# Layer 0's first two expert blocks fetch only two words per row, and the row buffers take blocks three to five at once

## The reference

```python
router_logits = x_flat @ gate_w
router_probs = jax.nn.softmax(router_logits, axis=-1)
expert_idx = jnp.argmax(router_probs, axis=-1)
expert_w = jnp.take_along_axis(router_probs, expert_idx[:, None], axis=1)[:, 0]
for e in range(NUM_EXPERTS):          # 8
    h = jax.nn.gelu(x_flat @ w1[e] + b1[e], approximate=False)   # 256 -> 1024
    y = h @ w2[e] + b2[e]                                        # 1024 -> 256
    out = out + jnp.where(expert_idx == e, expert_w, 0.0)[:, None] * y
```

## Time and profile before

| | |
|---|---|
| time before | 1849.13 us, median of 3 runs (1848.25 to 1849.85) |
| profiled execution | 1851.53 us |
| its span, first to last instruction | 1849.7 us |
| PE busy | 1609.4 us (87%) |
| DVE, ACT, POOL busy | 58%, 49%, 21% |
| mean granted PE clock | 0.943 of full speed |
| the experts stage of layer 0: from block 0's up projection to the end of the last down projection | 293.4 to 481.3 us |

### The profile page before, as it was taken

The page is one execution under the profiler, slowest core; times in us unless marked ns, Lnnn a source line. Parts: engine busy times, 40 slices in busy tenths (PEclk is TensorE's granted clock), DMA queues, the critical chain, the costliest instruction groups (busy, mean ns, idle before and its releaser), DMA issues.

```text
span 1849.7 us, 27965 instructions
## 1 busy us (share of the span) xinstructions
PE 1609.4 (87%) x9990; PEld 1215.6 (66%) x9998; DVE 1070.8 (58%) x3025; ACT 906.8 (49%) x2034; POOL 379.6 (21%) x480
## 2 busy tenths in 40 slices
PE   6999858999669999999958699999998779995566
PEld 5677637889556676767535667776675468894444
DVE  7767752222356666666667765555555534325887
ACT  4888821222136666666539455555554102223366
POOL 1000014111132323233240100000000342223734
PEclk9999989999879999999978899999999889997878
DMA  9000028889500000000000200000000338893001
GB/s 339 2 1 1 2 92 322 260 291 292 170 1 12 7 7 7 7 1 1 1 1 1 80 12 7 7 7 7 1 1 12 129 124 264 300 352 127 0 12 35
DMA packets 61625, 152.26 MB, mean 82 GB/s; under 512 B 8960, under 2 KB 39696, under 8 KB 55248
## 3 DMA queue, kind: packets, MB, share of 16 engines
q1 hardware_dynamic: 54096, 133.91, 21.9%
q0 software_dynamic: 5280, 14.47, 2.0%
q10 hardware_dynamic: 2112, 2.10, 0.4%
HBM read 133.89 MB, written 24.75 MB: 86 GB/s over the span
## 4 chain that ended last, share of the span: by engine, by line
PE 69%; DVE 15%; ACT 5%; POOL 4%; issue 4%; DMA 2%; POOLq 1%; SPq 0%; DVEq 0%; ACTq 0%
PE bank L1033 8%; PE bank L1456 8%; PE bank L976 8%; PE bank L1510 7%; PE bank L1523 6%; PE bank L1497 5%; PE bank L1460 5%; PE bank L1440 3%; PE bank L679 3%; PE bank L1862 2%; POOL sorted_h L1225 2%; PE bank L695 2%; PE bank L710 1%; ACT p1f L1578 1%; PE bank L616 1%
## 5 line engine op out<-in xcount | busy, mean ns | idle before, releaser
L1707 DVE TENSOR_REDUCE small<-bank 128x1 f32<-128x512 f32 x128 | 82.5, 686 | 108.7 <-PE bank L1510 108.7
L1052 ACT ACTIVATE e2a<-bank,WB 128x128 f32<-128x128 f32 x156 | 44.6, 368 | 178.7 <-PE bank L1033 178.7
L1703 DVE CUSTOM_DVE_ANT_0 p1f<-bank,p1f 128x512 f32<-128x512 f32 x128 | 83.2, 687 | 81.3 <-PE bank L1510 81.3
L1581 ACT ACTIVATE p2f<-bank,small 128x512 f32<-128x512 f32 x128 | 86.9, 683 | 86.2 <-DVE small L1707 86.1
L751 ACT ACTIVATE l<-l,small 128x256 f32<-128x256 f32 x256 | 108.9, 502 | 32.6 <-DVE small L817 32.2
L1578 ACT ACTIVATE p1f<-p1f,small 128x512 f32<-128x512 f32 x128 | 91.2, 714 | 67.9 <-DVE small L1703 67.5
L400 POOL TENSOR_SCALAR rs<-mv 128x4 f32<-128x4 f32 x16 | 3.6, 226 | 567.4 <-DVEq L230 551.7
L817 DVE CUSTOM_DVE_ANT_0 l<-bank,small 128x256 f32<-128x256 f32 x256 | 90.7, 420 | 13.4 <-PE bank L695 12.5
L1456 PE MATMUL bank<-WA,HT 128*128 128x256 f32 x384 | 93.1, 387 | 5.0 <-DVE p1f L1648 5.0
L1592 ACT ACTIVATE p2f<-bank 128x512 f32<-128x512 f32 x128 | 75.2, 598 | 40.5 <-PE bank L1497 39.0
L1052 ACT ACTIVATE e0a<-bank,WB 128x128 f32<-128x128 f32 x128 | 36.6, 368 | 112.7 <-PE bank L1033 112.7
(11 more groups left out here) (402 smaller groups left out, 3949.6 us busy)
## 6 DMA issues: line engine op xcount, KB each, us to landing
WB<-in_L2pack SPq DMA_DIRECT2D x39, 514.0 KB, 5.1
WB<-in_L2pack SPq DMA_DIRECT2D x39, 512.0 KB, 5.7
WB<-in_L0pack SPq DMA_DIRECT2D x16, 1028.0 KB, 6.4
WB<-in_L0pack SPq DMA_DIRECT2D x16, 1024.0 KB, 7.3
e0a<-in_L0pack SPq DMA_DIRECT2D x7, 1028.0 KB, 5.8
e0a<-in_L0pack SPq DMA_DIRECT2D x7, 1024.0 KB, 6.8
sorted_h<-in_blank SPq DMA_DIRECT2D x6, 1032.0 KB, 16.1
e2a<-sorted_h SPq DMA_DIRECT2D x39, 129.0 KB, 5.6
```

Source lines behind the costliest of these rows:

```text
L1581: ins = a.e.activation(P, k.bank(x), ACT.Exp, bias=self.mx[:, m:m + 1], accum_out=self.sm[:, m:m + 1])
```

## The change

In layer 0 only, blocks 0 and 1 no longer fetch their rows. `load_x` for them fetches words 256 and 257 of each row, 128 pieces of 8 bytes, into a small buffer of its own, `place_of`, counted by the flag `a_place`. POOL takes its index for these two blocks from there, and waits for `a_place`. DVE's two copies at block 2 are gone. Since `xs[0]` and `xs[1]` are free from the start, x3 and x4 no longer wait for `xt_d` 3, and SP issues x2, the two place fetches, x3 and x4 together ahead of block 3's down weights. x5 stays behind block 4's down weights. The counts of the row buffers' semaphores (`ax`) are one less in buffers 0 and 1.

```diff
--- before.py
+++ after.py
@@ -889,11 +889,14 @@
         self.beside = ()
         self.cleared = (k.setup.z0, 3) if tag == "e0" else (k.setup.z2, 5)
         self.a_b2 = k.dma("b2", 1)
-        self.ax = [k.dma(f"ex{i}", len(range(i, nt, 3))) for i in range(3)]
+        late = 3 if topk == 1 else 0
+        self.ax = [k.dma(f"ex{i}", len(range(i + late * (i < 2), nt, 3))) for i in range(3)]
         self.a1 = [k.dma(f"ew{i}", len(range(i, nt, nwb))) for i in range(nwb)]
         self.a2 = [k.dma(f"gather{4 + i}", len(range(i, nt, nwb))) for i in range(nwb)]
         self.sc = k.dma("scatter", n // 2), k.dma("ey0", n // 2)
         self.ay = [k.dma(f"ey{i}", len(range(i, nt, 3))) for i in range(3)]
+        if topk == 1:
+            self.a_place = k.dma("gather0", 2)
         self.ag = [k.dma(f"gather{i}", 1) for i in range(4 * topk)]
         f = k.flag
         nq = self.nq = nf // 4
@@ -902,7 +905,7 @@
         self.two = topk == 1
         if self.two:
             self.count256, self.seat = r(256, a=16, b=16), k.HT[:, :, :].rearrange("p c (t n) -> p (c t) n", n=256)
-            self.seated = f("p_cxn", 4)
+            self.seated, self.place_of = f("p_cxn", 4), r(4, i=2, n=2)
         self.routing = f("e_routing", 5)
         self.xt_t, self.xt_d = f("e_xt_t", nt), f("e_xt_d", nt)
         self.up_q, self.gel, self.dn, self.yc = f("up", nt * nq), f("gel", nt * nf), f("down", nt), f("y", nt)
@@ -1007,7 +1010,7 @@
     def turn_pe(self, t, i):
         k, x = self.k, self.xs[i % 3]
         T = k.bank(6 + i % 2)
-        t.wait_ge(self.ax[i % 3], i // 3 + 1)
+        t.wait_ge(self.ax[i % 3], i // 3 + (0 if self.two and i % 3 < 2 else 1))
         t.wait_ge(self.xt_d, i - 1)
         t.wait_ge(self.routing, self.GATED)
         if self.biased(i) is not None:
@@ -1198,10 +1201,6 @@
             return
         v.wait_ge(self.xt_t, i + 1)
         v.wait_ge(self.up_q, (i - 1) * self.nq)
-        if self.two and i == 2:
-            for j in range(2):
-                v.wait_ge(self.ax[j], 1)
-                v.e.tensor_copy(self.place[:, j:j + 1], self.xs[j][:, 256:257].bitcast(I32))
         for other in self.beside:
             other.block_dv(v, i, k.bank(6 + i % 2))
         if self.biased(i) is not None:
@@ -1227,8 +1226,9 @@
         for i in range(self.nt):
             g.wait_ge(self.yc, i + 1)
             if self.two and i < 2:
-                g.wait_ge(self.xt_d, 3)
-            g.e.indirect_dma_start(out=self.y, out_offset=bass.IndirectOffsetOnAxis(ap=self.place[:, i:i + 1], axis=0),
+                g.wait_ge(self.a_place, 2)
+            place = self.place_of[:, i, 0:1].bitcast(I32) if self.two and i < 2 else self.place[:, i:i + 1]
+            g.e.indirect_dma_start(out=self.y, out_offset=bass.IndirectOffsetOnAxis(ap=place, axis=0),
                                    in_=self.ys[i % 3], in_offset=None).then_inc(self.ay[i % 3].sem, 16)
 
     def load_up(self, s, i):
@@ -1251,8 +1251,11 @@
     def load_x(self, s, i):
         for h in range(2):
             s.wait_ge(self.sc[h], self.n // 2)
+        if self.two and i < 2:
+            s.e.dma_start(self.place_of[:, i, :], self.h[i * 128:(i + 1) * 128, 256:258]).then_inc(self.a_place.sem, 16)
+            return
         s.wait_ge(self.xt_t, i - 2)
-        s.wait_ge(self.xt_d, max(i - 2, 3) if self.two and i > 2 else i - 2)
+        s.wait_ge(self.xt_d, i - 2)
         s.e.dma_start(self.xs[i % 3], self.h[i * 128:(i + 1) * 128, :]).then_inc(self.ax[i % 3].sem, 16)
 
     def sp(self, s):
@@ -1266,12 +1269,12 @@
         start = 2 if self.two else 0
         if self.two:
             self.load_up(s, 3)
-            for i in range(3):
+            for i in (2, 0, 1, 3, 4):
                 self.load_x(s, i)
             self.load_down(s, 3)
             self.load_up(s, 4)
             self.load_down(s, 4)
-        for i in range(3 if self.two else 0, 4 + start):
+        for i in range(5 if self.two else 0, 4 + start):
             self.load_x(s, i)
         for i in range(start, self.nt):
             if i + self.nwb < self.nt:
```

## The result

The changed kernel took 1843.89 us, the median of 15 runs (1838.05 to 1847.67); the kernel before took 1850.51 us beside it (15 runs, 1845.32 to 1855.25). The ratio is 0.996 with a 95% interval of 0.995 to 0.9969: 0.4% faster, 7.4 us of 1850.5, between 5.7 and 9.3; the two medians lie 6.6 us apart. The forecast was 7.9 us.

A forecast was written before the change was run, and what follows sets the result against it. PE, busy 87% of the span, was taken to bound the kernel. 4.97 us of earlier turn plus 2.94 us of low clock gave 7.9 us, 1849.13 to 1841.2 us; range 1839.3 to 1844.6, the sum's own 1839.8 to 1842.7.

The forecast's parts named there:

- Block 3's turn: PE's turn of block 3 starts at 312.44 instead of 317.41, 4.97 us earlier, as its rows are no longer late.
- Block 3's up projection: On PE, starts at 313.78 and runs at full clock, 3.6 to 3.8 us instead of 6.75: 2.94 us more gained.
- The stage: Experts stage, block 0's up projection to the last down projection's end: ends 7.9 us earlier, later blocks still 8.17 us each.
- term (4): DVE loses two one-column copies ahead of block 2's turn copy; block 2's up projection starts 0.21 us earlier, at 308.79.
- x3's landing: Fetch of block 3's rows lands 4.2 us after issue, at 307.5, with 4.9 us of slack before PE wants it.
- the places: The two fetches of 128 8-byte pieces take 4.2 us like an x fetch, landing at about 307, while POOL still waits.
- The weights: Up and down weights of blocks 3 and 4 and block 5's up weights land before PE wants them.
- DMA's empty stretch: DMA's share of 0.00 in 322.00 to 325.50, a hole made by the stall, closes.
- Rival A: Clock drops all the same around PE's two pauses; block 3's up projection at half clock, 2.94 us, 1844.2 us; chance 0.06.
- Rival B: Stall stays because x3 or block 3's or 4's weights land late; 1849 us, or 1845 to 1849; chance 0.06.
- Rival C: Late places delay POOL's first scatter, then DVE and PE's down projections; slower, 1850 us or more; chance 0.02.
- The part behind the stage: From the end of the last down projection to the end of the span: the same to 1 us.

The follow-up runs named there:

- Run 1: The changed kernel with x3 and x4 issued behind block 4's down weights again: 1852.15 us, ratio to the kernel before 1.0014.
- run 2: The changed kernel with only x4 put back behind block 4's down weights, x3 early: 1842.09 us, one run.
- Run 3: The kernel before with 18 unused products on PE between block 2's up projection and block 3's turn: 1843.90 us, one run.
- run 11: The changed kernel with DVE's two one-column copies kept at the head of block 2's copies and POOL waiting for them: 1839.63 us, one run.
- Run 8: The changed kernel with 20 more fetches of 8-byte pieces ahead of x3, on the slower chip: 1864.00 us, one run.
- run 5: The changed kernel once more, no edit, on a slower chip: 1874.59 us, where the kernel before took 1874.09 us.
- run 4: The kernel before once more, no edit, for its profile: 1852.84 us, one run; its table sets the profiles' times behind the stage side by side.
- runs 5 to 8: The changed kernel unedited, with 680-byte place fetches, and with 8 and 20 more small fetches, on one slower chip: 1874.59, 1870.00, 1864.02 and 1864.00 us.

## Why the prediction was right

It said that the late x3 costs twice, 4.97 us until block 3's turn and 2.94 us of low clock behind it, and nothing else moves. Counted from the start of block 0's up projection, so that the two profiles can be laid over each other:

- *Block 3's turn* was to start 312.44 - 293.41 = 19.03 us in; it started at 312.21 - 293.09 = 19.12. Run 1 shows that SP's order makes it, run 2 that x3 does.
- *Block 3's up projection* was to start at 20.37 and did at 20.47, and took 3.81 us. Run 3 parts this term from the first: with the wait kept and PE busy in most of it, the 2.9 us come back alone.
- *The stage* was to last 179.95 us and lasted 180.04. The 0.09 us are term (4), sized at 0.21 and worth 0.12 (run 11).
- *x3's landing* was sized too long: 4.2 us from issue, measured 3.1 at most, and the places 3.5 instead of 4.2. What made them quicker no run tells apart. The slack was 6.6 us instead of 4.9. It was no term of the sum.
- *The weights* were never waited for, and DMA's empty stretch closed, as forecast. x5 went out at 308.59, took 9.0 us and was there for its turn at 325.38.
- *Rival A*, the clock, didn't come true in the changed kernel, with 0.85 us for each pause. Run 8 shows how near it is: with 2.02 us more between the two pauses the clock fell, while run 3 held it with 1.77.
- *Rival B* was excluded by 6.6 us of slack; run 8 shows it coming true where x3 goes out 10.8 us later than in run 5 on the same chip (3.75 us after the start of block 2's up projection, at 317.53, against 7.08 us ahead of it, at 313.50).
- *Rival C* wasn't reached: run 8 made POOL's first scatter 5.3 us late and PE's down projections didn't wait, but C needed places that land some 15 us later than they were expected to, and no run tried that.

One statement was wrong. The part behind the stage was to be the same to 1 us, and was 4.9 us shorter in the profiled execution. The sum didn't rest on it, and the table of run 4 shows that kernels which are alike there differ by as much; but as a test of the forecast it was set too tight. It took one execution's tail for a constant. For the same reason the three runs of the kernel before, 1848.25 to 1849.85, gave too small a picture of the spread: 15 runs reach from 1845.32 to 1855.25, with a median 1.4 us higher. The changed kernel's median, 1843.89 us, is 2.7 us above the forecast of 1841.2: 1.4 of it is that base, and 1.3 is that the medians lie 6.6 instead of 7.9 us apart.

So the place of the whole time in the range is in part luck. It lies above the 1839.8 to 1842.7 that the sum's own ends gave, and inside 1844.6 only because room had been left for rival A, which would have given 1844.2 and didn't come true. From the whole time alone A couldn't have been told from the forecast; it is the stage, right to 0.1 us, and block 3's up projection at full clock that decide. The chances have a slip of 0.01 too: the forecast's 0.86 and A's 0.06 are 0.92 already, not 0.91 with some of B.

Open is what holds PE and DVE ahead of block 0 on the slower chip of runs 5 to 8, and whether the change gains there: the one run of each kernel differs by 0.5 us, the changed one being the slower, where single runs differ by several.

## What to carry to other kernels

A transfer's time is read from what stands ahead of it in its queue: x3 took 8.4 to 9.6 us behind 3 MB of weights and about 3 us ahead of them, and all that kept it behind was a buffer held for one word per row. If a stall of PE is found, look at the duration of the products behind it too; here it added 2.9 us to the stall. And where the gain is 0.4%, compare the changed stage between profiles, where it is good to 0.1 us, before reading the whole: the whole differs by 5 us and more between executions of one kernel.

## What was not expected of the hardware

- A pause of PE cost a step of the clock in one execution and none in another: 28.96 against 27.59 us for the same stretch, though PE's pauses in it were the same to 0.01 us. The single runs of the changed kernel lie between 1838.05 and 1847.67 us.
- 20 fetches of 128 pieces of 8 bytes, issued 0.53 us apart on average, landed within 1.6 to 3.4 us each; in the place fetches pieces of 680 bytes took 4.7 us against 4.6 for 8 bytes.
- On one chip the kernel before took 1874.09 us in its one run, against about 1850 on the others. In run 5 the span was 36.1 us longer than in the first profile of the changed kernel: 10.2 us of it lie before the stage, 1.8 in it and 24.1 behind it. The cause isn't shown.
